# SP issues the shifted copies of the next image's queries ahead of the load of an image

## What is computed

```python
x = x + bn(dwconv(x, dw0_w, 1), dw0_bn)
x = ffn(x, ffn0_w1, ffn0_bn1, ffn0_w2, ffn0_bn2)
x = x + window_attn(x, qkv_w, qkv_bn, qdw_w, qdw_bn, attn_bias, proj_w, proj_bn)
x = x + bn(dwconv(x, dw1_w, 1), dw1_bn)
x = ffn(x, ffn1_w1, ffn1_bn1, ffn1_w2, ffn1_bn2)
...
# in window_attn, for 25 windows of 7 x 7 pixels:
q = bn(dwconv(q.reshape(Bw, NH * KD, H, W), qdw_w, 2), qdw_bn)   # 5 x 5 depthwise
attn = softmax(einsum('bhcn,bhcm->bhnm', q, k) * KD ** (-0.5) + bias)
out = einsum('bhdm,bhnm->bhdn', v, attn)
```

## Time and profile before

| | us |
| --- | --- |
| median of three runs | 4045.66 |
| lowest, highest | 4044.58, 4047.29 |
| the profiled execution | 4038.97 |
| its span (first to last instruction) | 4037.1 |

### The profile page before, as it was taken

The page is one execution under the profiler, slowest core; times in us unless marked ns, Lnnn a source line. Parts: engine busy times, 40 slices in busy tenths (PEclk is TensorE's granted clock), DMA queues, the critical chain, the costliest instruction groups (busy, mean ns, idle before and its releaser), DMA issues. The chain is left out here.

```text
span 4037.1 us, 80272 instructions
## 1 busy us (share of the span) xinstructions
PE 3184.8 (79%) x29652; PEld 2441.9 (60%) x29652; DVE 2720.9 (67%) x5162; ACT 2203.4 (55%) x3568; POOL 743.2 (18%) x869
## 2 busy tenths in 40 slices
PE   4787878787846658888888888888888886699993
PEld 2444445454535546767766777676767675587872
DVE  4767676767544448777777777777777775577763
ACT  2444454545524437666666666666656663477760
POOL 1000000000000000122122121121221122466660
PEclk9898999999967779989899888899889997899995
DMA  2344444445437689999999999999999994577768
GB/s 55 108 159 115 155 118 152 122 148 164 131 134 271 246 285 375 342 333 343 345 352 347 329 346 332 347 351 336 337 337 336 366 334 151 187 243 236 242 201 334
DMA packets 291012, 1023.89 MB, mean 254 GB/s; under 512 B 51620, under 2 KB 57520, under 8 KB 281574
## 3 DMA queue, kind: packets, MB, share of 16 engines
q1 hardware_dynamic: 273382, 985.62, 70.5%
q0 software_dynamic: 17280, 33.87, 2.3%
HBM read 486.25 MB, written 489.85 MB: 242 GB/s over the span
## 5 line engine op out<-in xcount | busy, mean ns | idle before, releaser
L1094 DVE CUSTOM_DVE_ANT_0 att_skewed<-att_score_ps,att_skewed 128x1024 f32<-128x1024 f32 x512 | 625.2, 1221 | 260.1 <-issue 243.2
L956 ACT ACTIVATE att_skewed<-att_skewed,att_neg_max 128x1024 f32<-128x1024 f32 x512 | 588.8, 1150 | 347.9 <-DVE att_neg_max L1094 347.0
L1212 PE MATMUL att_turn_ps<-att_ident,att_skewed 128*128 128x128 f32 x4096 | 592.0, 291 | 112.7 <-ACT att_skewed L956 110.4
L947 ACT ACTIVATE att_rows<-att_wide_ps 128x1152 f32<-128x1152 f32 x512 | 574.1, 1121 | 176.3 <-PE att_wide_ps L1176 174.9
L1212 PEld LDWEIGHTS att_turn_ps<-att_ident,att_skewed 128*128 128x128 f32 x4096 | 494.7, 149 | 280.3 <-ACT att_skewed L956 242.1
L1102 DVE COPY att_turned<-att_turn_ps 128x1024 f32<-128x1024 f32 x512 | 625.0, 1221 | 27.7 <-PE att_turn_ps L1212 27.4
L1176 PE MATMUL att_wide_ps<-att_ps,att_qs 98*128 98x128 f32 (+3 forms) x1920 | 452.9, 359 | 53.9 <-issue 29.6
L1204 PE MATMUL att_score_ps<-att_ks,att_qs 96*128 96x512 f32 x1024 | 379.7, 454 | 19.4 <-DVE att_neg_max L1094 17.9
L911 POOL DMA_INDIRECT expert_rows<-att_expert_rows,att_place x256 | 247.1, 965 | 786.6 <-DVE att_place L1052 701.2
L1176 PEld LDWEIGHTS att_wide_ps<-att_ps,att_qs 98*128 98x128 f32 x1920 | 324.5, 209 | 109.2 <-issue 67.7
L152 POOL DMA_INDIRECT expert_parts<-exp_parts,exp_rows x284 | 301.4, 1061 | 192.3 <-ACT exp_parts L183 126.3
(11 more groups left out here) (257 smaller groups left out, 5586.5 us busy)
## 6 DMA issues: line engine op xcount, KB each, us to landing
skewed_rows<-att_rows SPq DMA_DIRECT2D x512, 576.0 KB, 5.5
att_skewed<-skewed_rows SPq DMA_DIRECT2D x512, 512.0 KB, 6.9
expert_rows<-conv_pad SPq DMA_DIRECT2D x144, 520.0 KB, 10.9
exp_weights<-split_weights SPq DMA_DIRECT2D x71, 1028.0 KB, 7.0
att_qs<-queries SPq DMA_DIRECT2D x192, 128.0 KB
att_ks<-keys SPq DMA_DIRECT2D x192, 128.0 KB
exp_rows<-expert_rows SPq DMA_DIRECT2D x71, 260.0 KB, 2.8
sum_part<-expert_parts SPq DMA_DIRECT2D x32, 512.0 KB, 9.6
```

Of the source, the lines that this page charges most:

```text
L947: act.activation(rows[s % ROWS][:], wide_ps[:, 0:WIDE], ACT.Copy).then_inc(wide_read, 1)
L956: act.activation(skewed[r % RING][:], skewed[r % RING][:], ACT.Exp, bias=neg_max[:, k:k + 1], scale=-1.0, accum_out=sums[:, k:k + 1]).then ...
L1094: dve.tensor_tensor_reduce(skewed[r % RING][:], score_ps[:], skewed[r % RING][:], -SCALE, 3.0e38, ALU.add, ALU.min, neg_max[:, k:k + 1]).t ...
L1212: last = pe.transpose(turn_ps[:, t * P:(t + 1) * P], skewed[r % RING][:, t * P:(t + 1) * P], ident[:])
```

## The change

Two statements of SP's turn change places: the copies of image n+1 with their wait now stand ahead of the wait for `xp_ready` and the load of image n+3.

```diff
             def turn(n):
+                if not is_last(n):
+                    copies(n + 1)
                 if not (isinstance(n, int) and n >= NB - 3):
                     sp.wait_ge(xp_ready, n + 3)
                     sp.dma_start(x[:], x_dram[n + 3]).then_inc(x_loaded, 16)
-                if not is_last(n):
-                    copies(n + 1)
                 if not is_first(n):
                     store(n - 1)
                 sp.dma_start(xo[:], x_dram[n]).then_inc(xo_loaded, 16)
```

## The result

| | before | changed |
| --- | --- | --- |
| median, us | 4045.12 (4034.3 to 4047.29, 4 runs) | 3950.36 (3945.06 to 3951.96, 4 runs) |
| span of the profiled execution, us | 4037.1 | 3949.9 |

The ratio is 0.9769, 95% interval 0.9749 to 0.9789: 94.8 us less between the medians, 87.2 us less between the two profiled spans. The forecast was 3959.3, range 3946 to 3974.

What follows compares the result with a forecast made beforehand. TensorE and what it waits for were taken to set the convolution phase's turn length. Waits of 62.2 us plus 24.2 us of shorter convolutions made 86.4 us off, median 4045.66 to 3959.3, range 3946 to 3974.

Steps and rivals of the forecast that it cites:

- The wait goes to zero: TensorE's wait for the query copies before the convolution, turns 0 to 12: falls to zero, minus 62.2 us.
- The spare time of 4.4 us: Turn 7: the last query copy lands at 600.0, against the end of TensorE's keys at 604.4.
- The convolution gets shorter: Query convolution on TensorE, turns 0 to 12: 13.51 us each at full clock without idle time before it, minus 24.2 us.
- Rival A: The wait before the convolution goes but its slow start stays: only 62.2 us off, 3983.5 us; chance 0.06.
- The load of x: SP's load, moved behind the copies: starts about 2.7 us later, about 28 us to spare before VectorE reads it, no cost.
- What is late next: VectorE, idle 7.76 us before `conv_branch` in turn 13, isn't the bound; turns 1 to 12 look as turn 13.
- the low end of the range: All 13 turns as turn 13: 10.8 us less, 3948.5 us; with 2 us added for the runs' spread, 3946.
- B: Late copies or a late PSUM tile before the convolution take part of the wait's place: half the gain, 4003 us; chance 0.04.
- Rival C: A convolution never preceded by idle time is throttled to 1.2 GHz: 22.0 us each, 24 us slower, 4070 us; chance 0.01.
- D: On SP, the copies' own wait ends as late as `xp`, so the change does nothing: 4045 us; chance 0.01.

## Why the prediction was right

**The wait goes to zero.** Held in all 13 turns: 62.2 us predicted, 62.2 gone. The spare time of 4.4 us too: it was 4.7 in turn 8, and an extra load ahead of the copies, with landings up to 7.9 us, made no wait. What I had not separated is why the copies were late. I described it as lateness behind the wait for `xp` and gave the load no price of its own, although its row was there. The runs split it: of the 62.2 us, 30.6 go when only the load moves and 31.6 remain for the wait for `xp`. This split holds for that order only: with the wait for `xp` gone and a load still in front, all 62.2 us go. For the sum it made no difference, because both leave together. It would have for anyone who could move only the load.

**The convolution gets shorter.** 24.2 us predicted, 24.35 measured. That it is the idle time, and not the copies or the pads beside it, was an argument from turns 13 and 14; it is now shown from both sides, by filling the idle time (clock 1.00 with the DMA engines 98% busy) and by adding idle time without any late DMA (clock 0.50). Rival A, 3983.5 us, is out, and with it the working without this term: the rule of the Trainium skill (TensorE: Matmul & The Clock Gate, Part 1) that the ramp is under 1% of the span holds as a bound (24 of 4037 us), but it was 27% of what the change brought.

**The load of x.** Predicted to start about 2.7 us later with about 28 us to spare. It started 2.7 us after `xp` was ready, against 0.2 before, landed in 5.9 us instead of the 4.3 assumed, and had 27 us to spare. Putting it last took 15 us of that and cost nothing.

**What is late next.** Turns of 60.05 us were forecast from the mean of the other parts, and 778.19 / 13 = 59.86 came out; the term I took at nothing, the other parts of the turns, gave 2.3 us. VectorE's wait came out at 7.76 us in turn 8, just that of turn 13 before. Its mean fell to 156.2 / 16 = 9.8 us, not to the 8 forecast; without the longest wait, 34.9 us in both kernels, it is 8.1. Turn 0 took 57.6 us, outside the 59 to 61 forecast. The prediction had called turn 13 the one with the shortest other parts, 45.85 us, but in the trace of before those of turn 0 were shorter, 44.3 us (90.97 to 135.22). This bears on the low end of the range alone.

**The time.** The convolution phase's gain of 88.9 us is 2.5 more than the sum. The two profiled executions differ by 4038.97 - 3951.96 = 87.0 us, so the sum was nearly met there. The first pair of medians differs by 94.8, the second by 81.3, and the forecast's 86.4 lies between. The medians' distance from it is of the size of the attention phase's spread, but that this is its cause isn't shown. Rivals B, C and D have nothing in the profile after: no other wait in front of the convolution, a clock of 1.00 in it, copies issued 0.03 us after the queries. Rival C was also priced too low. It took 628 / 385 = 1.63 as the factor for a convolution at 1.2 GHz; 73 matmuls in 4 us at 1.00 against 40 at 0.50 give 1.8. By that (an estimate) the convolution would take 24.3 us and the kernel some 54 us more, not 24.

## What to carry to other kernels

In a queue that issues in order, put first what becomes ready first: a wait for something late holds back all behind it, and a large transfer ahead of a needed one costs again, where the needed one is late. Look in the trace of before for iterations at the edge of a loop that lack the step in question; here turn 13 was the experiment, already run, and read off the result. Where TensorE waits a few microseconds, price the wait and the slower work behind it; if the wait can't go, useless matmuls in its place can give back the second part, as they did here.

## What the runs showed that I had not expected

- Idle times of up to 1.86 us in front of the convolution left it at 13.4 to 13.5 us in every turn of these runs, those of 2.56 us and more always slowed it (to between 14.66 and 15.99 us), and between 1.95 and 2.48 us it went either way, not by length. In front of other products too the length did not decide alone: 2.24 us in front of the queries were followed by 2.36 us in one turn and 3.2 in the next, and 2.17 us in front of the FFN's second product by 5.37 instead of 3.67.
- A 512 KB load ahead of 2.65 MB of copies cost 2.35 us a turn, and a second one 1.3 us more; where the copies were early, a load ahead of them cost nothing.
- Useless work made a kernel faster: 50.7 us of added matmuls, 17.8 us less time.
- Removing one wait moved the slow start to the next one: with the windows cut first, the queries went from 3.8 to 4.5 us down to 2.36 in every second turn, and in the same turns the FFN's second product slowed to 5.32 us.
